# Self-attention in a decoder layer: VectorE's low part and its 16-bit copy, each in two halves with one maximum between them

## What is computed

```
qn = _rmsnorm(q, q_gamma) * dh ** (-0.5)
kn = _rmsnorm(k, k_gamma)
sim = jnp.einsum('bhid,bhjd->bhij', qn, kn)
attn = jax.nn.softmax(sim, axis=-1)
out = jnp.einsum('bhij,bhjd->bhid', attn, v)
```

## Time and profile before

| | |
|---|---|
| three runs, median (lowest to highest) | 2232.93 us (2232.64 to 2234.2) |
| the profiled execution, its own time | 2231.65 us |
| its span, first to last instruction | 2229.9 us |
| TensorE, busy share of the span | 96% |
| VectorE, ScalarE, GpSimd | 75%, 70%, 62% |
| mean granted clock of TensorE | 0.991 |

### The profile page before, as it was taken

How to read it: one execution, slowest core, us unless ns; L and a number is a source line. 1 busy time by engine, 2 the same in 40 slices (tenths; PEclk the granted TensorE clock), 3 DMA queues, 4 the chain that set the end, 5 groups by cost and what they waited for, 6 DMA issues and landing times. The chain is left out here.

```text
span 2229.9 us, 50857 instructions
## 1 busy us (share of the span) xinstructions
PE 2131.5 (96%) x19320; PEld 1210.9 (54%) x19320; DVE 1666.7 (75%) x2889; ACT 1555.7 (70%) x1763; POOL 1384.8 (62%) x982
## 2 busy tenths in 40 slices
PE   6999999999998899899999999999999988998999
PEld 3544666666665455444445456666666654554444
DVE  6998888888888666753379988888888885677522
ACT  4556999999997566631145589999999965666210
POOL 3425989898992586630234169989898826866210
PEclk9999999999999999999999999999999998999999
DMA  4210000000003102102122100000000030020000
GB/s 114 62 43 1 11 2 11 11 11 11 11 11 89 40 1 49 39 31 65 43 62 63 33 1 11 11 2 11 11 11 11 11 97 32 1 68 20 20 24 34
DMA packets 102422, 66.43 MB, mean 30 GB/s; under 512 B 75346, under 2 KB 75346, under 8 KB 102226
## 3 DMA queue, kind: packets, MB, share of 16 engines
q1 hardware_dynamic: 102226, 63.57, 12.8%
HBM read 46.69 MB, written 8.39 MB: 25 GB/s over the span
## 5 line engine op out<-in xcount | busy, mean ns | idle before, releaser
L627 POOL TENSOR_TENSOR qkn<-wide 128x1024 f16<-128x1024 f32 x420 | 883.9, 2133 | 113.0 <-PE bank L753 98.6
L967 DVE TENSOR_REDUCE sq<-bank 128x1 f32<-128x512 f32 x1024 | 676.2, 684 | 137.0 <-PE bank L696 132.7
L887 ACT ACTIVATE wide<-bank,shift 128x1024 f32<-128x1024 f32 x512 | 569.1, 1115 | 34.9 <-POOL qkn L627 15.6
L874 ACT ACTIVATE wide<-bank,shift 128x1024 f16<-128x1024 f32 x444 | 492.4, 1109 | 11.0 <-PE bank L712 7.8
L711 PE MATMUL bank<-q_hh,ko 128*128 128x512 f16 x1024 | 389.1, 380 | 7.4 <-ACT wide L887 7.1
L696 PE MATMUL bank<-ko,q_hh 128*128 128x512 f16 x1024 | 386.6, 379 | 8.9 <-DVE sq L967 6.7
L712 PE MATMUL bank<-q_lm,k_h 65*128 65x512 f16 x1024 | 389.0, 380 | 0.0
L735 PEld LDWEIGHTS bank<-v_hl,wide 128*128 128x128 f16 x4096 | 274.4, 97 | 122.0 <-DVE wide L1034 8.7
L735 PE MATMUL bank<-v_hl,wide 128*128 128x130 f16 (+1 forms) x4096 | 303.2, 212 | 5.2 <-DVE wide L1034 4.4
L753 PEld LDWEIGHTS bank<-v_hl,qkn 128*128 128x128 f16 x4096 | 189.0, 97 | 60.7 <-DVE qkn L1038 3.9
L753 PE MATMUL bank<-v_hl,qkn 128*128 128x65 f16 x4096 | 206.6, 193 | 3.5 <-DVE qkn L1038 3.5
(11 more groups left out here) (231 smaller groups left out, 4314.0 us busy)
## 6 DMA issues: line engine op xcount, KB each, us to landing
wide<-in_x SPq DMA_DIRECT2D x32, 256.0 KB, 2.7
q_lm<-in_x SPq DMA_DIRECT2D x32, 256.0 KB, 3.2
ko<-in_L_ffn_W SPq DMA_DIRECT2D x32, 256.0 KB, 4.1
q_hh<-q_hh SPq DMA_DIRECT2D x32, 128.0 KB, 2.6
ko<-k_h SPq DMA_DIRECT2D x32, 128.0 KB, 2.8
out<-bo_b SPq DMA_DIRECT2D x16, 256.0 KB, 2.0
out<-xbo_b SPq DMA_DIRECT2D x16, 256.0 KB, 2.0
q_lm<-sq SPq DMA_DIRECT2D x248, 0.2 KB, 4.8
```

Of the source, the lines that this page charges most:

```text
L627: pool.tensor_tensor(probs_l[:, p % 2, :], probs[:, p % 2, :], probs_h[:, p % 4, :], ALU.subtract).then_inc(pl_pool, 1)
L874: act.activation(probs_h[:, p % 4, :], SB[p % 2][:, :], ACT.Exp, bias=shift[:, 0:1])\
L887: act.activation(probs[:, p % 2, :], SB[p % 2][:, :], ACT.Exp, bias=shift[:, 0:1]).then_inc(p_ready, 1)
L967: dve.tensor_reduce(pm[:, s, k:k + 1], MB[k % 2], AX_X, ALU.max).then_inc(mx_free, 1)
```

## The change

`probs_low` and `probs_high` take a half (0 or 1) and work on 512 of the 1024 columns. The first half has the waits, the second raises the semaphore. The first half stands where the whole instruction stood, the second half one maximum later.

```diff
--- before.py
+++ after.py
@@ -973,19 +973,25 @@
                             dve.tensor_reduce(nm0[:, :, DH] if isinstance(r, int) and r == 0 else nm[:, s, :], pm[:, s, :].rearrange("p (a k) -> p a k", k=4), AX_X, ALU.max,
                                               negate=True).then_inc(nm_ready, 1)
 
-                        def probs_high(u):
-                            p = CAST
-                            dve.wait_ge(p_ready, (U0 + u) * PAIRS + p + 1)
-                            dve.tensor_reduce(probs_h[:, p % 4, :], probs[:, p % 2, :].rearrange("p (n a) -> p n a", a=1), AX_X,
-                                              ALU.max).then_inc(ph_dve, 1)
-
-                        def probs_low(u):
-                            p, G = DVE_PAIR, (U0 + u) * PAIRS + DVE_PAIR
-                            dve.wait_ge(p_ready, G + 1)
-
-                            dve.wait_ge(lo_done, G + 1)
-                            dve.tensor_tensor(probs_l[:, p % 2, :], probs[:, p % 2, :], probs_h[:, p % 4, :], ALU.subtract)\
-                                .then_inc(pl_dve, 1)
+                        def probs_high(u, half):
+                            p, cols = CAST, slice(half * CT, half * CT + CT)
+                            if half == 0:
+                                dve.wait_ge(p_ready, (U0 + u) * PAIRS + p + 1)
+                            copy = dve.tensor_reduce(probs_h[:, p % 4, cols],
+                                                     probs[:, p % 2, cols].rearrange("p (n a) -> p n a", a=1), AX_X, ALU.max)
+                            if half:
+                                copy.then_inc(ph_dve, 1)
+
+                        def probs_low(u, half):
+                            p, G, cols = DVE_PAIR, (U0 + u) * PAIRS + DVE_PAIR, slice(half * CT, half * CT + CT)
+                            if half == 0:
+                                dve.wait_ge(p_ready, G + 1)
+
+                                dve.wait_ge(lo_done, G + 1)
+                            low = dve.tensor_tensor(probs_l[:, p % 2, cols], probs[:, p % 2, cols], probs_h[:, p % 4, cols],
+                                                    ALU.subtract)
+                            if half:
+                                low.then_inc(pl_dve, 1)
 
                         def o_out(u):
                             first = u // (2 * CH) * (CH * TPC * P) + u % CH * (TPC * P) + u // CH % 2 * DH
@@ -1052,10 +1058,11 @@
                                 reduce_max(u + LA, k, s)
                                 if 4 <= k < 4 + 2 + WIDE and not first:
                                     output(u - 1, 1 - s, k - 4)
-                                if k == (6 if first else 2 * DVE_PAIR + 1):
-                                    probs_low(u)
-                                if k == (9 if first else 2 * CAST - 1):
-                                    probs_high(u)
+                                for half in range(2):
+                                    if k == (6 if first else 2 * DVE_PAIR + 1) + half:
+                                        probs_low(u, half)
+                                    if k == (9 if first else 2 * CAST - 1) + half:
+                                        probs_high(u, half)
                             negate_max(u + LA, s)
 
                         dve.tensor_copy(eye16[:, :], ident[:, :]).then_inc(e_eye, 1)
```

## The result

The changed kernel takes 2312.53 us (median; 2310.38 to 2313.63, 4 runs), the kernel before in the same comparison 2233.35 us (2232.64 to 2234.2). The ratio is 1.0357, interval 1.0344 to 1.0370: 79.2 us slower. The profiled execution took 2310.38 us, 78.7 us more than the one of before.

What follows compares the result with a forecast made beforehand. A closed chain through VectorE, ScalarE, GpSimd and TensorE, with about 0.1 us of slack at each joint, was taken to bound the kernel. 60 units x 1.35 = 81 us on 2231.65 gave 2313 us, range 2268 to 2330.

Steps and rivals of the forecast that it cites:

- Work: VectorE's halves of 512 elements in the attention loop: 0.72 us for the low part, 0.68 for the copy.
- Low part: VectorE's low part of pair 4 ends 0.69 us late; ScalarE's exponential of pair 6 ends at 412.32, not 411.63.
- Copy: VectorE's 16-bit copy of pair 6 ends at 414.26, against 412.88: 1.38 us late.
- GpSimd and the next unit: GpSimd's pair 6 waits for the copy, the next unit's exponentials follow; period 17.57 us, 1.37 longer, 1.35 taken.
- Sum: 60 units x 1.35 = 81 us, added to the profiled 2231.65 us, gives 2313 us.
- The port: VectorE's two-input subtraction and GpSimd's SBUF reads exclude each other; GpSimd's pair 5 is held to about 411.0, costing nothing.
- upper bound: Halves at their long ends plus 0.1 us for a first half held by GpSimd: 1.55 us, 93 us in all, 2325.
- GpSimd first: Rival: GpSimd's pair 5 starts ahead of the low part's second half; 138 us more, 2451 us; chance 0.04.
- One delay swallowed: Rival: GpSimd or ScalarE makes up one of two delays, 0.7 us each; 42 us, 2274 us; chance 0.09.
- Faster: Rival: maxima 10 and 12 leave VectorE earlier, so TensorE's maximum 14 need not wait; 7 us, 2224 us; chance 0.04.
- What would show it: Signs: GpSimd idle about 1.4 us before pair 6, ScalarE waiting 0.65 us, TensorE waiting, loop some 40 us longer.
- The clock: Rival of a slower TensorE clock, called without weight: TensorE would idle 1.37 of 17.57 us, 8%; no chance given.

Runs made afterwards that it cites:

- one-input run: The changed kernel with VectorE's low part of pair 4 replaced by a one-input reduction: 2305.75 us, ratio 1.0316.
- two-maxima kernel: Against the kernel before, only the low part of pair 4 is in halves, with two maxima between them; copy whole: 2486.49 us, ratio 1.1130.
- two lone splits: Two kernels, each keeping one split of the change: only `probs_low` in halves, 2275.41 us; only `probs_high` in halves, 2270.70 us.
- kernel with adjacent halves: The changed kernel with each second half directly behind its first, no maximum between them: 2245.30 us, ratio 1.0055.

## Why the prediction was right

2313 us was forecast, 2312.53 measured. The steps, each counted from the start of the scores of pair 6 (408.52 before, 407.19 after):

- *Work.* 120 halves of the low part last 0.768 us on average where 0.72 was taken (0.68 alone, 0.82 when GpSimd's pair 3 is still running), 120 of the copy 0.681 where 0.68 was.
- *Low part.* Its end went from 1.96 to 409.83 - 407.19 = 2.64 us: 0.68 late, forecast 0.69. ScalarE's exponential went with it, from 2.00 to 2.67. The end is right partly by luck. The forecast had maximum 10 wait for its product, 0.63 us behind the start of the first half; in fact the product was done 0.1 us earlier, and the maximum waited for the first half itself, which GpSimd's pair 3 (to 408.08) held up, so it began 0.74 behind. That is 0.11 too little, and three terms were 0.12 too much: the start of the first half (0.62 behind the scores, not 0.67), the maximum (0.60, not 0.63) and the second half (0.68, not 0.72).
- *Copy.* Its end went from 4.36 to 412.89 - 407.19 = 5.70: 1.34 late, forecast 1.38. Of the 0.04, 0.03 is the maximum between the halves, which holds VectorE for 0.60 us (411.61 to 412.21) and not 0.63, and 0.01 came with the low part.
- *GpSimd and the next unit.* The exponential of pair 0 begins 8.00 after the scores, before 6.67. From there to the end of that of pair 4 it is 424.66 - 415.19 = 9.47 us, forecast 9.48: ScalarE has no gap there in which a delay could be made good. The period is 17.52, forecast 17.57, taken 17.55.
- *Sum.* 60 x 1.32 = 79.2 us, which is what was measured. That it fits to the tenth is luck too, since a batch's first unit costs more than 1.3 us. From GpSimd's low part of pair 0 to that of pair 7, 21.84 us in both batches before, it takes 23.37 in the first and 24.29 in the second. In both the second half lasts 2.01 us, behind GpSimd; in the second batch the granted clock falls as well, and this unit takes 0.9 us more:

```profile
181.52:204.89 23.37, 19.16 (x174) 10.06 (x175) 19.61 (x31) 14.85 (x15) 12.93 (x6) 1.00 0.02 1
1324.42:1348.71 24.29, 20.68 (x174) 10.74 (x175) 19.70 (x31) 15.76 (x15) 12.94 (x7) 0.93 0.01 1
```

- *The port.* That GpSimd's pair 5 would be held by 0.17 us in the loop and that this would cost nothing holds for pair 5 (2.30 us against 2.13, and it then waits 1.21 us for the copy). What the one-input run gives back beyond the first units, 0.06 us a unit, goes with the first half's 0.82 us, 0.68 there; that first half was allowed for only in the upper bound.
- *The rivals.* GpSimd first: this does not happen in the loop and does happen in the first unit of each batch, where its place was not looked at. Its price leaves out the clock, which took some 70 us more in the two-maxima kernel, where it was made to happen. One delay swallowed: refuted by the sum of the two lone splits. Faster: TensorE's maximum 14 is not earlier. Its product begins 412.35 - 407.19 = 5.16 us behind the scores, before 5.02, because VectorE comes 0.68 us later to the copy that stands in front of maximum 12; and TensorE's weight loads wait 0.51 us each time for a maximum, before 0.38.
- *What would show it.* The two pieces and ScalarE's 0.65 us are there, and so is the second idle time of GpSimd, but 1.2 and not 1.4 us long, as pair 5 in front of it lasts 0.17 longer. The loops are longer by 38.3 and 39.3 us (GpSimd's first low part to pair 5 of the last unit touched), some 40 having been forecast. TensorE does not stand at the scores of pair 6, where a wait was forecast: its waiting is spread over the scores of the pairs, some 0.08 us each.
- *The clock.* 0.992 after, 0.991 before: no rival of weight, as argued. In the loop TensorE shows 10.3 us of idle time in 447, 2% and not the 8% that the argument allowed for. For the first unit of the second batch, with a granted clock of 0.93, it did not hold, and the two-maxima kernel, with 0.950 over the run, shows that the clock can cost much more where TensorE stands longer.

## What to carry to other kernels

Where one semaphore stands behind both halves, splitting an instruction gives no consumer anything sooner, and whatever is put between the halves is added to its latency in full. What decides is whether the instruction's consumers have slack, not whether its engine has: here VectorE was idle for 2 us of each 16, and every joint of the chain through it had about 0.1 us or less, so 0.6 us of a maximum became 0.66 us of each unit (with some 0.06 for the split itself), twice. Read a closed chain by following it once round to the same instruction of the next unit; if the sum is the period, each delay on it counts as often as the loop runs.

## What the runs showed of the hardware

- VectorE's subtraction of two SBUF tensors and GpSimd's wait for each other, and the turn goes to whoever begins first, per instruction: 0.68 us became 2.42 (GpSimd 0.26 us ahead), 2.01 and, for two adjacent halves, 3.21; a reduction with one input in the same place took 0.68. The Trainium skill, SBUF — State Buffer, "Who interferes with whom", says that a VectorE instruction with two SBUF inputs contends with a GpSimd instruction that reads SBUF, one with a single input does not, and the order of issue decides who waits; these runs agree. That a split gives the turn away in the middle is what they add. So these two engines meet not only at semaphores, as the description of the core has it.
- TensorE's clock went to the 1.2 GHz level after idle times of 1.03 and 0.82 us within 2.3 us, in the kernel with two maxima between the halves; after 1.11 and 0.82 us in the unit before, it did not. In a batch's first unit TensorE stands 1.68 us for a maximum in the changed kernel, and the granted clock was 1.00 in the first batch and 0.93 in the second; with 2.60 us, in the kernel with adjacent halves, it was 0.93 in both. With single waits of 0.2 us, in the loop of the changed kernel, it stayed at 1.00. What decides between two like idle times no run here shows.
